# Second stage of a conditional MLP taken row by row, with one product of 512 and one of 256 columns per unit and two sums per tile

## Chip, core and metric

The kernel runs on one core of a Trainium2 chip. The metric is the device time of one execution in microseconds, median of the runs. Work is split over TensorE (PE, matrix products into PSUM), VectorE (DVE), ScalarE (ACT), GpSimd (POOL) and SyncE (SP, which issues nearly all DMAs).

## The reference, cut

32 rows of 256 tokens and 256 features; 1024 hidden features; 192 shared outputs and 64 outputs of one of 16 experts, chosen per row; all in fp32.

```python
h = jax.nn.gelu(jnp.einsum('bnd,hd->bnh', x, fc1_w) + fc1_b, approximate=False)
shared = jnp.einsum('bnh,sh->bns', h, fc2_w) + fc2_b
We = experts_w[indices]
be = experts_b[indices]
expert_x = jnp.einsum('bnh,bph->bnp', h, We) + be[:, None, :]
return x + jnp.concatenate([shared, expert_x], axis=-1)
```

## The kernel before

Every operand of a product is kept as a high part (rounded to TensorE's fp32r type) and a low part (what the rounding left). A product of two such operands is three products of TensorE: high x high, high x low, low x high.

**Blocks and stages.** A block is two rows: 512 tokens, four token tiles of 128. There are 16. The first stage (fc1, gelu) makes hidden features, transposed, in pairs of chunks (a chunk is 128 features, eight of them, four pairs, "quarters" below). Blocks 0 and 1 do it plainly, in `conv_chunk`: six products of 512 columns a chunk. Blocks 2 to 15 do it with seven groups of block products instead of eight (P1 to P7, `product`, six products of 256 columns each), in two rounds a block (`g` = 0 and 1, `t` counts them, 28 rounds). Between the groups ScalarE copies P1 and P5 out (`s1_copy`, `s5_copy`) and VectorE adds (`add_c11`, `add_v`, `add_c12`, `add_c22`); P4 is added last, so `product4(t - 1)` stands in the next round and waits for `add_c22`. ScalarE's gelus (`upper_pair`, `lower_pair`) leave two pairs a round in `gelu`; `pair_high` rounds them into `ht`, and POOL's `pair_lo` makes the low parts (in block 1 VectorE does it, `plain_low(4)` to `plain_low(7)`).

**The second stage** (`fc2_units(n, r, first, count)`, r a quarter) is cut into units: one token tile and one chunk, three products of 256 columns, weights from `w2t`. A quarter has eight units, two chunks by four tiles. Its sums stand in `acc_ps`, two banks, one for each row of the block. In `w2t` the columns of expert 0 stand left of the shared ones and those of expert 1 right, so each row reads 256 neighbouring columns. The units of block n - 1 fill the gaps of block n's rounds, two or three between each two groups. After the fourth quarter `drain` adds the sums to `resid`, which holds x plus the biases (`residual`, POOL). The sums of a row have one bank, drained while TensorE is at the other row.

**What sets the order.** All of it is written out by hand, one program per engine, with semaphores. The expert weights of a block are turned in VectorE (`experts_square`) into PSUM bank pair `tr_ps`, rounded by ScalarE (`experts_high`), and their low part made by VectorE (`experts_low`), in halves of four chunks for both rows at once. x of a later block goes the same way (`x_square`, `b_copy`, `x_high`, `x_low`, `x_sums_first`, `x_sums_last`, POOL's `x_sums_lo`). At the start POOL also forms four sums of first-stage weights (`weight_sum`), which VectorE turns (`s_square`), ScalarE rounds (`s_high`) and VectorE completes (`s_low`). SP's queue has, in this order, x of block 0, weights, experts 0, x of block 1 in pieces, expert biases 0, x of block 2, experts 1, and later the shared bias.

## Time and profile before

| | us |
|---|---|
| median of 3 runs (lowest to highest) | 363.62 (363.24 to 364.08) |
| the profiled execution | 363.34 |
| its span, first to last instruction | 361.5 |
| PE busy | 356.4 |
| ACT, DVE, POOL busy | 243.6, 224.0, 222.2 |

A product's busy time in the trace reaches into the next product's (a 256-column product is shown with 0.28 us while the products start 0.12 us apart), so distances from start to start are read, not durations. The granted clock of TensorE is 0.998 of full speed over the span. One execution's start times are in the rows further down, counted from the span's start.

### The profile page before, as it was taken

The numbers are of one execution on the slowest core, as the hardware profiler recorded it, in microseconds if no ns is written. First come the engines' busy times: TensorE is split into PE (matmuls) and PEld (weight loads), VectorE is DVE, ScalarE is ACT, GpSimd is POOL, SyncE is SP. The second block draws the span as 40 slices with busy tenths as digits, with TensorE's granted clock in tenths as the row PEclk, the third lists the DMA queues.
The fourth block names the chain that finished last, engine by engine and source line by source line (L and its number), as shares of the span: only waits on it lengthen the run. The fifth ranks groups of instructions, "written<-read, shape, count | busy, mean of one in ns | idle before, by whom it ended". The sixth has DMA issues, their size and how long they took to land.

```text
span 361.5 us, 7842 instructions
## 1 busy us (share of the span) xinstructions
PE 356.4 (99%) x2863; PEld 350.3 (97%) x2863; DVE 224.0 (62%) x367; ACT 243.6 (67%) x410; POOL 222.2 (61%) x100
## 2 busy tenths in 40 slices
PE   8999999999999999999999999999999999999996
PEld 6898999999999999999999999999999999999996
DVE  1797993937758285683937658395673938653241
ACT  3794865757849576694857759576794857757560
POOL 0079824676655677565676655677565577655381
PEclk9999999999999999999999999999999999999999
DMA  8869856361703426044261603526052321403011
GB/s 202 183 160 117 156 143 150 126 160 45 175 22 116 127 69 173 31 124 89 82 160 52 168 25 109 132 82 162 29 140 74 94 91 58 126 18 100 2 58 58
DMA packets 70447, 37.86 MB, mean 105 GB/s; under 512 B 43530, under 2 KB 70410, under 8 KB 70410
## 3 DMA queue, kind: packets, MB, share of 16 engines
q1 hardware_dynamic: 69792, 36.85, 40.8%
q10 hardware_dynamic: 618, 0.53, 0.6%
q8 instruction: 22, 0.36, 0.4%
q14 instruction: 15, 0.12, 0.1%
HBM read 28.97 MB, written 8.39 MB: 103 GB/s over the span
## 4 chain that ended last, share of the span: by engine, by line
PE 95%; issue 2%; POOL 1%; ACT 1%; DVE 0%; POOLq 0%
PE fc_ps L985 37%; PE acc_ps L1017 16%; PE acc_ps L1021 16%; PE acc_ps L1019 16%; PE fc_ps L961 6%; PE fc_ps L930 1%; POOL ht L353 1%; PE tr_ps L924 1%; PE fc_ps L968 1%; ACT ht L510 0%; ACT gelu L536 0%; DVE work L794 0%; DVE resid L819 0%; ACT w1t L430 0%; PE acc_ps L924 0%
## 5 line engine op out<-in xcount | busy, mean ns | idle before, releaser
L353 POOL TENSOR_TENSOR ht<-gelu,ht 128x1024 fp32r<-128x1024 f32 x60 | 144.5, 2408 | 121.3 <-ACT ht L510 121.3
L985 PE MATMUL fc_ps<-xt,w1t 128*128 128x256 f32 x1176 | 173.2, 283 | 0.0
L985 PEld LDWEIGHTS fc_ps<-xt,w1t 128*128 128x128 f32 x1176 | 155.3, 192 | 0.1
L1017 PE MATMUL acc_ps<-w2t,ht 128*128 128x256 f32 x512 | 144.9, 283 | 0.2 <-POOL ht L353 0.2
L1019 PE MATMUL acc_ps<-w2t,ht 128*128 128x256 f32 x512 | 144.9, 283 | 0.0
L1021 PE MATMUL acc_ps<-w2t,ht 128*128 128x256 f32 x512 | 144.9, 283 | 0.0
L1017 PEld LDWEIGHTS acc_ps<-w2t,ht 128*128 128x128 f32 x512 | 98.3, 192 | 0.6 <-POOL ht L353 0.3
L1019 PEld LDWEIGHTS acc_ps<-w2t,ht 128*128 128x128 f32 x512 | 98.3, 192 | 0.3
L1021 PEld LDWEIGHTS acc_ps<-w2t,ht 128*128 128x128 f32 x512 | 98.3, 192 | 0.0
L510 ACT ACTIVATE ht<-gelu 128x1024 fp32r<-128x1024 f32 x64 | 68.0, 1062 | 3.3
L496 ACT ACTIVATE work<-fc_ps 128x512 f32<-128x512 f32 x28 | 16.8, 600 | 57.4 <-PE fc_ps L985 57.4
L778 DVE TENSOR_TENSOR work<-fc_ps,work 128x512 f32<-128x512 f32 x28 | 19.4, 691 | 54.6 <-PE fc_ps L985 45.8
L346 POOL TENSOR_TENSOR resid<-resid,bias 128x1024 f32<-128x1024 f32 x16 | 38.9, 2432 | 1.5 <-DMA resid<-in_x 0.8
L787 DVE TENSOR_TENSOR work<-fc_ps,work 128x512 f32<-128x512 f32 x28 | 19.2, 687 | 32.0 <-PE fc_ps L985 32.0
L361 POOL TENSOR_TENSOR xt<-work,xt 128x1024 fp32r<-128x1024 f32 x14 | 33.6, 2402 | 7.7 <-ACT xt L500 7.7
L450 ACT ACTIVATE w2t<-tr_ps 128x512 fp32r<-128x512 f32 x32 | 18.8, 590 | 29.0 <-PE acc_ps L1021 29.0
L536 ACT ACTIVATE gelu<-work,b 128x512 f32<-128x512 f32 x56 | 37.1, 712 | 0.7 <-DVE work L794 0.7
L794 DVE TENSOR_TENSOR work<-fc_ps,work 128x512 f32<-128x512 f32 x28 | 19.3, 691 | 12.8 <-PE fc_ps L985 11.2
L548 ACT ACTIVATE gelu<-work,b 128x256 f32<-128x256 f32 x56 | 25.2, 501 | 0.0
L709 DVE TENSOR_TENSOR w2t<-tr_ps,w2t 128x512 fp32r<-128x512 f32 x32 | 22.0, 690 | 4.7 <-ACT w2t L450 3.2
L802 DVE TENSOR_TENSOR work<-fc_ps,work 128x512 f32<-128x512 f32 x28 | 19.1, 683 | 7.2 <-PE fc_ps L985 7.2
L553 ACT ACTIVATE gelu<-fc_ps,b 128x256 f32<-128x256 f32 x56 | 23.3, 469 | 0.0
(57 smaller groups left out, 279.5 us busy)
## 6 DMA issues: line engine op xcount, KB each, us to landing
pieces<-in_L_cond_experts_w SPq DMA_DIRECT2D x128, 64.0 KB, 2.0
out<-resid SPq DMA_DIRECT2D x32, 256.0 KB, 3.0
...
```

Of the source, the lines that this page charges most:

```text
L346: nc.gpsimd.tensor_tensor(rows, rows, bias[:, par, :, :].unsqueeze(2).to_broadcast([P, R, T, OUT]), ALU.add).then_inc(resid_ready, 1)
L353: nc.gpsimd.tensor_tensor(ht[:, slot, LO, :, :].rearrange("p k t -> p (k t)"), gelu[:, q % GELUS, :, :].rearrange("p k t -> p (k t)"), ht[ ...
L361: nc.gpsimd.tensor_tensor(xt[:, n % 2, X_T1:X_T4 + 1, LO, :], t_sum, xt[:, n % 2, X_T1:X_T4 + 1, HI, :].bitcast(FP32), ALU.subtract).then_ ...
L510: nc.scalar.activation(ht[:, q % PAIRS, HI, :, :].rearrange("p k t -> p (k t)"), gelu[:, q % GELUS, :, :].rearrange("p k t -> p (k t)"), A ...
L536: nc.scalar.activation(gelu[:, q % GELUS, j, :], upper[:, j, :], ACT.Gelu, bias=b1[:, k:k + 1]).then_inc(up_gelu, 1)
L548: nc.scalar.activation(gelu[:, q % GELUS, j, SEQ:2 * SEQ], c22[:, j, :], ACT.Gelu, bias=b1[:, k:k + 1]).then_inc(c22_gelu, 1)
L553: nc.scalar.activation(gelu[:, q % GELUS, j, 0:SEQ], fc1_ps[:, BANK_A[t % 2], j * SEQ:(j + 1) * SEQ], ACT.Gelu, bias=b1[:, k:k + 1]).then_ ...
L709: nc.vector.tensor_tensor(expert_columns(LO, ks), tr_ps[:, half, :].rearrange("p (k b c) -> p b k c", k=HALF, b=R), expert_columns(HI, ks) ...
L985: last = nc.tensor.matmul(fc1_ps[:, dst, j * SEQ:(j + 1) * SEQ], w1t[:, w, wv, ms], xt[:, n % 2, o, xv, :], start=(fresh and j == 0 and at ...
L1017: nc.tensor.matmul(dst, h_hi_t, w_hi, start=(r == 0 and u % (2 * T) == 0), stop=True, skip_group_check=True)
L1019: nc.tensor.matmul(dst, h_hi_t, w_lo, start=False, stop=True, skip_group_check=True)
L1021: last = nc.tensor.matmul(dst, h_lo_t, w_hi, start=False, stop=True, skip_group_check=True)
```

## The change

**Second stage by rows.** `fc2(i, first, count)` replaces `fc2_units`; i counts quarters of a row, eight a block: four of row 0, then four of row 1. A quarter has four units, two chunks by two tiles. A unit is two products: the high part of h against high and low weights side by side (512 columns, from two runs of 256 in `w2t`), and the low part of h against the high weights (256 columns) into the second half. So a tile has a bank of its own with two sums of 256, and `drain` adds both, one tile at a time, 8 adds for row 0 and 4 for row 1, where 2 and 1 stood. Both rows use the same two banks: the first units of a row wait, tile by tile, until the row ahead is drained.

**Storage.** `ht` has six pairs instead of four, since row 1 reads a pair later; `w1_piece` moves into `work`; the shared bias is kept once (`bias`), the expert biases apart (`e_bias`), and a residual is four instructions for a block, two for each row.

**Order.** In a round `product4(t - 1)` and both quarters i and i + 1 (i = 6 + 4 t) stand ahead of P1; then P1, P2, P5, P6 follow without units between; then three units, P3, two, P7, three. At the start six quarters of block 0 stand among the plain chunks (one chunk at the end without), the last two lead the first round; behind the last P4 stand ten quarters, forty units (thirty before). VectorE's and ScalarE's queues move the expert weights to halves by row; `drain(0, 0)` stands ahead of `plain_low(4)`; `x_square` or `experts_square` stands between `add_c12` and `add_c22`; `x_square` of block 3 stands ahead of `plain_low(7)`; ScalarE does `b_copy` and `x_high` ahead of `upper_pair` and `s1_copy`. POOL does `residual(0, 0)` ahead of all low parts, and SP loads the biases of block 0 ahead of the x pieces of block 1.

```diff
-        ht = sbuf("ht", [P, PAIRS, 2, 2, TOK], FP32R)
+        ht = sbuf("ht", [P, SLOTS, 2, 2, TOK], FP32R)
...
-        bias = sbuf("bias", [P, 2, R, OUT])
+        bias = sbuf("bias", [P, SHARED])
+        e_bias = sbuf("e_bias", [P, 2, R, PART])
...
+        w1_piece = work[:, 0:2048].rearrange("p (q k j) -> p q k j", q=Q, k=K)
...
-        def drained_at(n, b):
-
-            return 3 * n + 2 + b
+        def additions(b):
+
+            return 2 - b
+
+        def drained_at(n, b, t):
+
+            return 12 * n + 8 * b + 2 * additions(b) * (t + 1)
+
+        def fc2_end(n, b, r):
+
+            return R * PAIRS * n + PAIRS * b + r + 1
...
             numbers = load_experts(0)
+            load_expert_bias(0, numbers)
+            sp.dma_start(bias[:, :], fc2_b.rearrange("(o n) -> o n", o=1).to_broadcast([P, SHARED]))\
+                .then_inc(b2_loaded, 16)
             load_x_pieces(1)
...
+                    rows[:, :, 0:SHARED], rows[:, :, 0:SHARED],
+                    bias[:, :].unsqueeze(1).to_broadcast([P, T, SHARED]),
                     ALU.add).then_inc(resid_ready, 1)
+                nc.gpsimd.tensor_tensor(
+                    rows[:, :, SHARED:OUT], rows[:, :, SHARED:OUT],
+                    e_bias[:, par, b, :].unsqueeze(1).to_broadcast([P, T, PART]),
+                    ALU.add).then_inc(resid_ready, 1)
...
+            residual(0, 0)
             for r in range(PAIRS):
...
-            residual(0)
-            residual(1)
+            residual(0, 1)
+            for b in range(R):
+                residual(1, b)
...
             def drain(n, b):
-                if b == 0:
-                    dve.wait_ge(acc_filled, n + 1)
-                else:
-                    dve.wait_ge(fc2_pair, PAIRS * (n + 1))
-                dve.wait_ge(resid_ready, n + 1)
-                dst = resid[:, n % 2, b * T:(b + 1) * T, :]
-                src = acc_ps[:, b, :].rearrange("p (t o) -> p t o", t=T)
-                if b == 0:
-                    nc.vector.tensor_tensor(dst[:, :, 0:SHARED], src[:, :, PART:OUT],
-                                            dst[:, :, 0:SHARED], ALU.add).then_inc(drained, 1)
-                    nc.vector.tensor_tensor(dst[:, :, SHARED:OUT], src[:, :, 0:PART],
-                                            dst[:, :, SHARED:OUT], ALU.add).then_inc(drained, 1)
-                else:
-                    nc.vector.tensor_tensor(dst, src, dst, ALU.add).then_inc(drained, 1)
+
+                dve.wait_ge(resid_ready, 4 * n + 2 * b + 2)
+                for t in range(T):
+                    if t == 0:
+                        dve.wait_ge(tile_filled, R * n + b + 1)
+                    else:
+                        dve.wait_ge(fc2_done, fc2_end(n, b, PAIRS - 1))
+                    dst = resid[:, n % 2, b * T + t, :]
+                    for v in (HI, LO):
+                        src = acc_ps[:, t, v * OUT:(v + 1) * OUT]
+                        if v == LO:
+                            dve.wait_ge(drained, drained_at(n, b, t) - additions(b))
+                        if b == 0:
+                            nc.vector.tensor_tensor(dst[:, 0:SHARED], src[:, PART:OUT],
+                                                    dst[:, 0:SHARED], ALU.add)\
+                                .then_inc(drained, 1)
+                            nc.vector.tensor_tensor(dst[:, SHARED:OUT], src[:, 0:PART],
+                                                    dst[:, SHARED:OUT], ALU.add)\
+                                .then_inc(drained, 1)
+                        else:
+                            nc.vector.tensor_tensor(dst, src, dst, ALU.add).then_inc(drained, 1)
...
             experts_square(1, 0)
+            drain(0, 0)
             plain_low(4)
...
-            def fc2_units(n, r, first, count):
-
+            def fc2(i, first, count):
+
+                n, b, r = i // (R * PAIRS), i // PAIRS % R, i % PAIRS
                 q = PAIRS * n + r
                 for u in range(first, first + count):
-                    t, j = u // 2, u % 2
-                    b = t // T
+                    j, t = u // T, u % T
                     k = chunk_of(q, j)
                     if u == 0:
                         wait_h_lo(pe, q)
-                        if r % 2 == 0:
-                            pe.wait_ge(e_lo, 2 * n + r // 2 + 1)
-                        if q == 0:
+                        if r == 0:
+                            pe.wait_ge(e_lo, R * n + b + 1)
+                        if i == 0:
                             pe.wait_ge(w2_lo, 4)
-                    if r == 0 and n >= 1 and u in (0, T * 2):
-                        pe.wait_ge(drained, drained_at(n - 1, b))
-                    dst = acc_ps[:, b, (t % T) * OUT:(t % T + 1) * OUT]
-                    ts = slice(t * P, (t + 1) * P)
-                    h_hi_t = ht[:, q % PAIRS, HI, j, ts]
-                    h_lo_t = ht[:, q % PAIRS, LO, j, ts]
-                    w_hi = w2t[:, HI, k, fc2_columns(b)]
-                    w_lo = w2t[:, LO, k, fc2_columns(b)]
-                    nc.tensor.matmul(dst, h_hi_t, w_hi, start=(r == 0 and u % (2 * T) == 0),
-                                     stop=True, skip_group_check=True)
-                    nc.tensor.matmul(dst, h_hi_t, w_lo, start=False, stop=True,
-                                     skip_group_check=True)
-                    last = nc.tensor.matmul(dst, h_lo_t, w_hi, start=False, stop=True,
-                                            skip_group_check=True)
-                    if u == 7:
-                        last.then_inc(fc2_pair, 1)
-                    elif r == PAIRS - 1 and u == 3:
-                        last.then_inc(acc_filled, 1)
+                    if r == 0 and j == 0 and i > 0:
+
+                        pe.wait_ge(drained, drained_at(n - (1 - b), 1 - b, t))
+                    ts = slice((b * T + t) * P, (b * T + t + 1) * P)
+                    nc.tensor.matmul(acc_ps[:, t, :].rearrange("p (v o) -> p v o", v=2),
+                                     ht[:, q % SLOTS, HI, j, ts], w2t[:, :, k, fc2_columns(b)],
+                                     start=(k == 0), stop=True, skip_group_check=True)
+                    last = nc.tensor.matmul(acc_ps[:, t, OUT:2 * OUT],
+                                            ht[:, q % SLOTS, LO, j, ts],
+                                            w2t[:, HI, k, fc2_columns(b)],
+                                            start=False, stop=True, skip_group_check=True)
+                    if u == 3:
+                        last.then_inc(fc2_done, 1)
+                    elif r == PAIRS - 1 and u == 2:
+                        last.then_inc(tile_filled, 1)
...
-            fc2_units(0, 0, 0, 8)
+            fc2(0, 0, 4)
+            fc2(1, 0, 4)
             pe.wait_ge(x1_lo, D)
             conv_chunk(K)
-            for at in range(6):
-                fc2_units(0, 1 + at // 2, at % 2 * 4, 4)
-                conv_chunk(K + 1 + at)
+            conv_chunk(K + 1)
+            for at in range(4):
+                fc2(2 + at, 0, 4)
+                conv_chunk(K + 2 + at)
+            conv_chunk(2 * K - 2)
             conv_chunk(2 * K - 1)
 
             for n in range(PLAIN, BLOCKS):
                 for g in range(GROUPS):
                     t = group(n, g)
                     a = BANK_A[t % 2]
...
+                    i = 6 + 4 * t
+
+                    if t > 0:
+                        product4(t - 1)
+                    fc2(i, 0, 4)
+                    fc2(i + 1, 0, 4)
...
+            for i in range(6 + 4 * (LAST_T + 1), R * PAIRS * BLOCKS):
+                fc2(i, 0, 4)
```

TensorE, the head of the first round (t = 0), before; `fc_ps<-xt,w1t` are the groups P1, then P2, `acc_ps<-w2t,ht` the products of units:

```order
L985 MATMUL fc_ps<-xt,w1t 128x256 [waits conv_gelu]
L985 MATMUL fc_ps<-xt,w1t 128x256 x5
L1017 MATMUL acc_ps<-w2t,ht 128x256 [waits e_lo,plain_lo]
L1019 MATMUL acc_ps<-w2t,ht 128x256
L1021 MATMUL acc_ps<-w2t,ht 128x256
...
L985 MATMUL fc_ps<-xt,w1t 128x256 [waits c22_added]
L985 MATMUL fc_ps<-xt,w1t 128x256 x5
```

and now, from the last unit ahead of P1 to the first unit behind P6:

```order
L1043 MATMUL acc_ps<-w2t,ht 128x512
L1046 MATMUL acc_ps<-w2t,ht 128x256
L1015 MATMUL fc_ps<-xt,w1t 128x256 [waits conv_gelu,xb_lo]
L1015 MATMUL fc_ps<-xt,w1t 128x256 x5
L1015 MATMUL fc_ps<-xt,w1t 128x256 [waits conv_gelu]
L1015 MATMUL fc_ps<-xt,w1t 128x256 x5
L1015 MATMUL fc_ps<-xt,w1t 128x256 [waits s_lo,xt_lo]
L1015 MATMUL fc_ps<-xt,w1t 128x256 x5
L1015 MATMUL fc_ps<-xt,w1t 128x256 [waits s_lo,s1_copied]
L1015 MATMUL fc_ps<-xt,w1t 128x256 x5
L1043 MATMUL acc_ps<-w2t,ht 128x512 [waits drained,e_lo,plain_lo]
L1046 MATMUL acc_ps<-w2t,ht 128x256
```

The units between the groups are gone; the first units behind P6 wait (`drained`) for the tiles of the row ahead.

VectorE, behind the transposes of block 1's experts in the start (`L701`), before; `ht<-gelu,ht` is `plain_low`, `tr_ps<-w_in` is `s_square`, `w2t<-tr_ps,w2t` is `experts_low`:

```order
L701 STREAM_TRANSPOSE tr_ps<-pieces 128x4x4x32 [waits e_loaded1,t_added,xb_lo]
L729 TENSOR_TENSOR ht<-gelu,ht 128x1024 [waits h_hi]
L665 STREAM_TRANSPOSE tr_ps<-w_in 128x512 [waits s_added]
L709 TENSOR_TENSOR w2t<-tr_ps,w2t 128x2x4x64 [waits e_hi]
L671 TENSOR_TENSOR w1t<-tr_ps,w1t 128x512 [waits s_hi]
```

and now:

```order
L719 STREAM_TRANSPOSE tr_ps<-pieces 128x2x8x32 [waits e_loaded1,t_added,xb_lo]
L835 TENSOR_TENSOR resid<-acc_ps,resid 128x192 [waits tile_filled,resid_ready]
L838 TENSOR_TENSOR resid<-acc_ps,resid 128x64
L835 TENSOR_TENSOR resid<-acc_ps,resid 128x192 [waits drained]
L838 TENSOR_TENSOR resid<-acc_ps,resid 128x64
L835 TENSOR_TENSOR resid<-acc_ps,resid 128x192 [waits fc2_done]
...
L745 TENSOR_TENSOR ht<-gelu,ht 128x1024 [waits h_hi]
L683 STREAM_TRANSPOSE tr_ps<-w_in 128x512 [waits s_added]
L726 TENSOR_TENSOR w2t<-tr_ps,w2t 128x8x64 [waits e_hi]
L689 TENSOR_TENSOR w1t<-tr_ps,w1t 128x512 [waits s_hi]
```

Eight adds of the first drain, which wait for the fourth quarter of row 0 (`tile_filled`, `fc2_done`), have come ahead of all of this.

POOL, the head of its queue, before (`pair_lo`, `x_sums_lo`):

```order
L379 AFFINE_SELECT ident<-ident 128x128
L353 TENSOR_TENSOR ht<-gelu,ht 128x1024 [waits h_hi] x4
L361 TENSOR_TENSOR xt<-work,xt 128x4x256 [waits xt_hi]
```

and now:

```order
L394 AFFINE_SELECT ident<-ident 128x128
L356 TENSOR_TENSOR resid<-resid,bias 128x2x192 [waits b2_loaded,be_loaded0,x0_tr,x0_loaded0]
L360 TENSOR_TENSOR resid<-resid,e_bias 128x2x64
L368 TENSOR_TENSOR ht<-gelu,ht 128x1024 [waits h_hi] x4
L376 TENSOR_TENSOR xt<-work,xt 128x4x256 [waits xt_hi]
```

The residual of row 0, with its wait for both biases, stands ahead of the four low parts.

## Rows read from the trace of the kernel before

**Rows 1.** Page of the profile: busy time of each engine; the chain that ended last.

```profile
PE 356.4 (99%) x2863; PEld 350.3 (97%) x2863; DVE 224.0 (62%) x367; ACT 243.6 (67%) x410; POOL 222.2 (61%) x100
...
PE 95%; issue 2%; POOL 1%; ACT 1%; DVE 0%; POOLq 0%
```

**Rows 2.** Timeline, 149.8 to 151 us: start, us, engine, line, operation, out<-in.

```profile
149.89 0.28 PE L1017 MATMUL acc_ps<-w2t,ht 128*128 128x256 f32 x1
...
150.25 0.28 PE L1017 MATMUL acc_ps<-w2t,ht 128*128 128x256 f32 x1
...
150.42 0.53 DVE L814 TENSOR_TENSOR resid<-acc_ps,resid 128x384 f32<-128x384 f32 x1
...
150.88 0.27 DVE L816 TENSOR_TENSOR resid<-acc_ps,resid 128x128 f32<-128x128 f32 x1
```

**Rows 3.** TensorE by stretch, line 961 alone: us, PE busy (count), weight loads, clock, DMA, GB/s.

```profile
11.40:21.04 9.64, 9.64 (x42) 7.78 (x42) 1.00 0.78 171
23.92:25.30 1.38, 1.38 (x6) 0.94 (x6) 1.00 0.47 118
```

**Rows 4.** Timeline: the one wait of TensorE after 21 us.

```profile
343.15 2.41 POOL L353 TENSOR_TENSOR ht<-gelu,ht 128x1024 fp32r<-128x1024 f32 x1 [5.63 <-ACT ht L510]
...
345.67 0.19 PEld L1017 LDWEIGHTS acc_ps<-w2t,ht 128*128 128x128 f32 x1 [0.34 <-POOL ht L353]
...
345.89 0.28 PE L1019 MATMUL acc_ps<-w2t,ht 128*128 128x256 f32 x1
```

**Rows 5.** VectorE's groups by form: busy us, mean ns of one | idle before.

```profile
L720 DVE STREAM_TRANSPOSE tr_ps<-pieces 128x512 f32<-128x512 f32 x30 | 19.7, 700 | 0.1
...
L709 DVE TENSOR_TENSOR w2t<-tr_ps,w2t 128x512 fp32r<-128x512 f32 x32 | 22.0, 690 | 4.7 <-ACT w2t L450 3.2
...
L724 DVE TENSOR_TENSOR work<-tr_ps,work 128x256 f32<-128x256 f32 x28 | 11.7, 418 | 0.5
...
L819 DVE TENSOR_TENSOR resid<-acc_ps,resid 128x512 f32<-128x512 f32 x16 | 10.9, 680 | 0.7 <-PE acc_ps L1021 0.7
...
L729 DVE TENSOR_TENSOR ht<-gelu,ht 128x1024 fp32r<-128x1024 f32 x4 | 6.6, 1658 | 1.6 <-ACT ht L510 1.4
...
L816 DVE TENSOR_TENSOR resid<-acc_ps,resid 128x128 f32<-128x128 f32 x16 | 4.4, 274 | 0.0
```

**Rows 6.** Timeline: a seventh product of a round and the add behind it.

```profile
159.97 0.88 PE L985 MATMUL fc_ps<-xt,w1t 128*128 128x256 f32 x6
...
160.89 0.69 DVE L802 TENSOR_TENSOR work<-fc_ps,work 128x512 f32<-128x512 f32 x1 [0.51 <-PE fc_ps L985]
```

**Rows 7.** Timeline: a weight load that waited for VectorE.

```profile
8.84 1.29 DVE L659 TENSOR_TENSOR w1t<-acc_ps,w1t 128x512 fp32r<-128x512 f32 x2 [0.45 <-ACT w1t L430]
...
10.18 0.19 PEld L968 LDWEIGHTS fc_ps<-xt,w1t 128*128 128x128 f32 x1 [0.30 <-DVE w1t L659]
```

**Rows 8.** Timeline: ScalarE's copy of P5, and the low part that follows in POOL.

```profile
156.21 0.60 ACT L496 ACTIVATE work<-fc_ps 128x512 f32<-128x512 f32 x1 [0.33 <-PE fc_ps L985]
...
159.55 2.41 POOL L353 TENSOR_TENSOR ht<-gelu,ht 128x1024 fp32r<-128x1024 f32 x1 [2.93 <-ACT ht L510]
```

**Rows 9.** Timeline of the start, SP and POOL.

```profile
12.95 2.02 SPq L269 DMA_DIRECT2D pieces<-in_x  x4
...
18.16 2.41 POOL L353 TENSOR_TENSOR ht<-gelu,ht 128x1024 fp32r<-128x1024 f32 x1 [16.68 <-ACT ht L510]
...
21.23 2.41 POOL L353 TENSOR_TENSOR ht<-gelu,ht 128x1024 fp32r<-128x1024 f32 x1 [0.66 <-ACT ht L510]
...
27.30 2.65 POOL L353 TENSOR_TENSOR ht<-gelu,ht 128x1024 fp32r<-128x1024 f32 x1 [0.58 <-ACT ht L510]
```

**Rows 10.** DMA view, 26 to 42 us: issues, KB each, median us to landing.

```profile
bias<-in_L_cond_fc_b SPq DMA_DIRECT2D x1, 384.0 KB, 12.0
```

**Rows 11.** Timeline: a VectorE instruction with two operands in SBUF beside one of POOL.

```profile
29.90 2.40 POOL L361 TENSOR_TENSOR xt<-work,xt 128x1024 fp32r<-128x1024 f32 x1
...
31.26 2.13 DVE L729 TENSOR_TENSOR ht<-gelu,ht 128x1024 fp32r<-128x1024 f32 x1 [1.44 <-ACT ht L510]
```

More of the change, by code:

```diff
@@ L272, in store @@
             def store(n, b):
[L273 removed]
+                sp.wait_ge(drained, drained_at(n, b, T - 1))
                 ts = slice(b * T, (b + 1) * T)
@@ L306, in _ @@
             load_x_pieces(3)
-            sp.wait_ge(e_sq, 2)
+            sp.wait_ge(e_sq, R)
             numbers = load_experts(2)
-            sp.wait_ge(resid_ready, 1)
+            sp.wait_ge(x_sq, 2 * D)
+            load_x_pieces(4)
+            sp.wait_ge(resid_ready, 4)
             load_expert_bias(2, numbers)
-            for n in range(1, BLOCKS):
-                if n >= 2:
-                    store(n - 2, 1)
+            store(0, 0)
+            for n in range(PLAIN, BLOCKS):
                 if n + 3 <= LAST:
@@ L408, in _ @@
                     if g == 1:
-                        residual(n)
+                        for b in range(R):
+                            residual(n, b)
             pair_lo(pair_at(LAST_T, 0))
@@ L587, in _ @@
             conv_chunk(4)
-            for half in range(2):
-                experts_high(0, half)
+            for b in range(R):
+                experts_high(0, b)
             conv_chunk(5)
@@ L837, in _ @@
             dve.wait_ge(w1_lo, 2 * D)
-            for half in range(2):
-                experts_square(0, half)
-            for half in range(2):
-                experts_low(0, half)
+            for b in range(R):
+                experts_square(0, b)
+            for b in range(R):
+                experts_low(0, b)
             dve.wait_ge(e_lo, 2)
@@ L870, in _ @@
             s_square(2)
-            experts_square(1, 1)
             s_low(2)
-            drain(0, 0)
-            drain(0, 1)
             plain_low(6)
+            dve.wait_ge(s_lo, 4)
+            for d in range(D):
+                x_square(PLAIN + 1, d)
             plain_low(7)
```

203 lines of the change are left out of this document (98 added, 105 removed).

## The prediction

> **What bounds the kernel now.** I read the page's shares first: TensorE is busy 356.4 us of a span of 361.5, and the chain that ended last is 95% TensorE [rows 1]. A busy TensorE can still be slowed by its products' own gaps, so next comes the pitch, from start to start. Three products of the second stage start 0.12 us apart, so one unit (one token tile, one hidden chunk, three products of 256 columns) takes 150.25 - 149.89 = 0.36 us [rows 2]. The 512-column products of the start take 9.64 / 42 = 0.2295 us each, six of them 1.38 us [rows 3]. Twice 256 columns cost 0.240 us and once 512 cost 0.2295: a product has a fixed part of some 0.010 us. From 21.04 us, the end of the first of those stretches, TensorE has one hole, 0.34 us at 345.67 [rows 4]. So nothing but TensorE sets the time, every product saved counts in full, and every new hole counts in full too.
>
> **What the change does, part by part.** The sum is made against the profiled execution, 363.34 us (span 361.5, 1.84 around it); the median of the runs is 363.62.
>
> *Products.* A unit becomes one product of 512 and one of 256: 0.2295 + 0.120 = 0.3495 us instead of 0.360. There are 512 units (the 512 of L1017): 512 x 0.0105 = **-5.4**. The trace holds no product whose moving columns lie in two runs; by the nearest rows a unit lies between 0.360 (two runs cost what two products cost) and 3 x (0.2295 - 0.120) = 0.3285 (no fixed part left), a saving of 0 to 16.1. I take 0.3495 because L961 streams the same 512 columns in the same type.
> The Trainium skill ("TensorE: Matmul & The Clock Gate", Back-to-back issue gap) gives N / 2.4 plus about 2.5 ns. By it a unit saves one fixed part of 2.5 ns, as an estimate 1.3 us in all, and the sum below would be 4.1 us higher. The rows differ: 256 columns take 13 ns, not 2.5, over their 107.
>
> *The rounds of the loop.* A round has seven groups of six products (0.72 each) and 16 units: 5.04 + 5.76 = 10.80 before, 5.04 + 5.59 = 10.63 now. The new order is safe where it leaves more than a microsecond: the sums of a row are drained under P1, P2, P5, P6 (2.88 us); eight adds for row 0 take 4 x 0.34 + 4 x 0.21 = 2.2 us, four for row 1 take 4 x 0.42 = 1.7 (widths between and beside [rows 5]). One place is tight. Only three units now stand between P7 and P4, where three units, P1 and two more stood. P7 started at 159.97 and VectorE's add began at 160.89, ended at 161.58, 1.61 after P7's start [rows 6]. VectorE to weight load takes 10.18 - 10.13 = 0.05 [rows 7], so P4's load can start at 1.66; TensorE gets there at 0.72 + 3 x 0.3495 - 0.12 = 1.65. The transposes placed between the two adds fit: third add 0.69 and 0.70 of transpose end 0.1 before P7 has. I take 0.02 a round, 28 rounds: **+0.6**, between 0 and 0.1 a round.
> Costed at nothing: the second quarter of a round now leads, so its low part is wanted earlier. ScalarE's copy of P5 started at 156.21 and that low part ended at 161.96, 5.75 later [rows 8]; the copy now comes 5.9 into a round (P4, eight units, P1, P2, P5, 0.2 of ends), so the part is ready 1.0 into the next one, and wanted at 0.72 + 1.40 - 0.21 = 1.9. That 0.9 is its cover. The doubled adds and the split residuals fill idle time of VectorE (62% busy) and POOL (61%) [rows 1]; the row-wise expert weights keep their size.
>
> *The start.* Here cover is lost. Before, quarter 1's low part (POOL, 21.23 to 23.64) had until 25.30, since eight units and a chunk stood ahead of it [rows 9]. Now four units do: TensorE arrives at 21.04 + 1.40 = 22.44. And POOL first does `residual(0, 0)`, which waits for both biases. SP issues them from 12.95 on, some 1 us for the expert rows; the shared bias took 12.0 us to land at 384 KB [rows 10], a quarter of it is left, so 3.0 by proportion: it lands near 17.3. Half a residual in two instructions is about 1.4 us (an estimate from 2.40 for 1024 columns). POOL is free at 18.7 to 18.9 instead of 18.16, quarter 1's low part ends at 23.8, and POOL to product takes 345.77 - 345.56 = 0.21 [rows 4] (345.77 is 0.12 ahead of the second product's start). So quarter 1 starts at 24.0, 1.5 late; if the bias lands 2.5 later, 4.0 late. (The x pieces of block 1, put back by the biases by some 1.5 us in SP's queue, are wanted for chunk 8, which is 1.5 later itself.) Chunk 8 ends at 26.8; the low part of quarter 3 started 2.0 after chunk 8's end (27.30 against 25.30), now 28.8, ends 31.2; quarter 3 runs 31.4 to 32.8. Without waits its end is 21.04 + 16 x 0.3495 + 3 x 1.38 = 30.8.
> Behind it hangs VectorE. `drain(0, 0)` stands ahead of `plain_low(4)` in its queue, so four low parts of block 1, eight transposes and low parts of the weight sums, the expert low part, two transposes and five small sums of block 3 all wait for quarter 3; and quarter 8 waits for `drain(0, 1)` behind them all. From the first add: 2.2 for the first drain, 4 x 1.66, 6 x 0.70, 5 x 0.69, 5 x 0.42, then 1.7 for the second drain: 20.3 us [rows 5]. An instruction that waits for nothing starts 0.07 before the one ahead has ended (150.42 + 0.53 against 150.88 [rows 2]); 28 such steps take off 2.0, waits on ScalarE, above all for the fourth weight sum, add 0.7: 19.0. The first tile's sums are full 0.18 before quarter 3 ends, 32.65, so the second drain ends at 51.65 and TensorE sees it at 51.8. TensorE alone would be there at 21.04 + 32 x 0.3495 + 8 x 1.38 + 2.88 + 0.35 = 46.5. **+5.3**. A low part of two operands in SBUF took 2.13 when POOL was at work and ended 1.09 after POOL's instruction did (31.26 + 2.13 against 29.90 + 2.40 [rows 11]); with POOL out of the way it is 1.1, so the term lies between 3.1 (four at 1.1) and 7.8 (bias 2.5 late).
> The Trainium skill ("SBUF — State Buffer", Who interferes with whom) says that a VectorE instruction with two SBUF inputs and a GpSimd instruction that reads SBUF exclude each other for a whole instruction; the row agrees. By it the new adds, with one operand in PSUM, are not slowed.
>
> *The end.* Ten quarters stand behind the last P4, with no group of products between a row's last quarter and the next row's first. Both tiles must be drained there. Row 1 of block 14: the tile is full 0.18 before the quarter ends, two dependent adds 0.87, hops of 0.04 (160.85 to 160.89 [rows 6]) and 0.17 (0.05 to the load, 0.12 to its product): 0.9 of waiting, then 0.4 more for tile 1 (its adds take 0.83 more, TensorE does one unit of 0.35): **+1.3**. Row 0 of block 15 has four adds a tile, 1.05 and 0.9: **+1.6**. The last drain is four adds, 1.63 from 0.14 before the last slot ends; one of 0.68 stood there (L819), starting 0.19 after it: **+0.6**. The hole at 345.67 goes: **-0.3**.
>
> Sum: -5.4 + 0.6 + 5.3 + 1.3 + 1.6 + 0.6 - 0.3 = +3.7, so 363.34 + 3.7 = **367.0 us**.
>
> **Rivals.**
> *The gaps vanish (faster).* While 512 columns stream, the next weights load in full; if the fixed part is what a load costs that doesn't fit under its stream, a unit takes 0.3285 and 10.7 more are saved: 356.3. It beats the kernel before from 0.341 a unit down. For it: no row shows long and short products in turn. Against it: the 42 long products in a row had the same room for their loads and took 0.2295, not 0.219. Chance 0.12.
> *VectorE's queue doesn't decide the start (no difference).* If the second drain is there when quarter 8 is, only the 2.0 us up to quarter 3 remain, 3.3 less: 363.7. It needs a chain of 15.7 instead of 19.0 us. Chance 0.10.
> *The biases land late.* +2.5: 369.5. For it: the 12.0 us of the same transfer. Against it: it is now a quarter as long and issued behind a queue that was nearly empty. Chance 0.09.
> *P4 waits in every round.* If the transpose ahead of the add comes late, by a quarter of a microsecond, 28 x 0.23 more: 373.4. Against it: 0.1 us of room by the rows. Chance 0.09.
> *Only a small fixed part is saved*, 2.5 ns a unit instead of 10.5: 371.1. Chance 0.03, since the 512-column rows speak against it. The Trainium skill's gap, cited above, is that case.
>
> **How the numbers follow.** My sum, 367.0, has 0.57. With the second and third rival that is 0.76, and the lower half of the fourth's prices belongs to it too, some 0.80; the range that they span is 363.6 to 370.4, which takes in the bounds of the start (3.1 to 7.8) as well. Below 0.2% (0.7 us), which is about what a measurement of this kernel can tell from no change: faster 0.14 (the first rival and a little of my own case), same 0.10 (the second), slower 0.76.
>
> **What the profile after would show.** Units 0.35 apart (right) or 0.33 or 0.36 (wrong). A round of 10.63 to 10.65 and no wait for the fourth add. Holes of TensorE at 21 to 24 us released by POOL's low part, at some 31 us, at 48 to 52 us released by VectorE's adds or its ScalarE successors, 5 us in all; VectorE without idle time from 33 to 51 us. Two holes after the last P4, 1.3 and 1.6. If there are no holes at 48 to 52 us, the chain of VectorE was wrong; if the rounds differ from 10.6, the pitch or the tight place was.

## The result, and the profile after

The changed kernel takes 370.15 us (369.82 to 371.26, median of 4 runs) against 363.82 for the kernel before in the same session: a ratio of 1.0182, 95% interval 1.0156 to 1.0208. It is slower, as forecast, but by 6.3 us instead of 3.4. The profiled execution took 370.4 us, its span is 368.4.

The page of the kernel after, shares and TensorE's clock (the answer to [rows 1]; the last line is the clock in 40 slices of 9.2 us):

```profile
PE 357.8 (97%) x2351; PEld 324.8 (88%) x2351; DVE 254.0 (69%) x511; ACT 246.9 (67%) x410; POOL 235.0 (64%) x148
...
PEclk9999989999999999999999999999999999999999
```

TensorE is the bound still, with 512 products fewer and a busy time that is 1.4 us longer. The sixth slice of the clock was a 9 before. TensorE's timeline, after (start, time, line, [idle before, releaser]): the first and the last row are P1, P2, P5 and P6 of the second and of the last round; the two at 82.55 and 93.24 are one round apart, with units between (where [rows 2] had three products 0.12 apart).

```profile
61.16 3.04 PE L1015 MATMUL fc_ps<-xt,w1t 128*128 128x256 f32 x24
...
82.55 3.04 PE L1015 MATMUL fc_ps<-xt,w1t 128*128 128x256 f32 x24
85.42 0.40 PE L1043 MATMUL acc_ps<-w2t,ht 128*128 128x512 f32 x1
85.65 0.28 PE L1046 MATMUL acc_ps<-w2t,ht 128*128 128x256 f32 x1
85.77 0.40 PE L1043 MATMUL acc_ps<-w2t,ht 128*128 128x512 f32 x1
...
93.24 3.04 PE L1015 MATMUL fc_ps<-xt,w1t 128*128 128x256 f32 x24
...
339.19 3.04 PE L1015 MATMUL fc_ps<-xt,w1t 128*128 128x256 f32 x24
```

One unit shows 0.35, but the round tells it closer: from 61.16 to 339.19 there are 26 rounds, 10.693 us each, and (10.693 - 7 x 0.72) / 16 = 0.3533. No wait stands in these 26 rounds.

The same view at the start (first the long stretch of the plain chunks) and behind the last P4:

```profile
12.47 9.81 PE L991 MATMUL fc_ps<-xt,w1t 128*128 128x512 f32 x42
...
24.76 0.50 PE L1043 MATMUL acc_ps<-w2t,ht 128*128 128x512 f32 x1 [0.73 <-POOL ht L368]
...
49.05 0.97 PE L1015 MATMUL fc_ps<-xt,w1t 128*128 128x256 f32 x6 [0.42 <-ACT work L507]
51.53 0.47 PE L1043 MATMUL acc_ps<-w2t,ht 128*128 128x512 f32 x1 [1.51 <-DVE resid L842]
...
52.23 0.80 PE L1043 MATMUL acc_ps<-w2t,ht 128*128 128x512 f32 x1
...
350.82 0.47 PE L1043 MATMUL acc_ps<-w2t,ht 128*128 128x512 f32 x1 [0.78 <-DVE resid L842]
357.91 0.47 PE L1043 MATMUL acc_ps<-w2t,ht 128*128 128x512 f32 x1 [0.92 <-DVE resid L838]
358.74 0.50 PE L1043 MATMUL acc_ps<-w2t,ht 128*128 128x512 f32 x1 [0.24 <-DVE resid L838]
...
364.03 0.28 PE L1046 MATMUL acc_ps<-w2t,ht 128*128 128x256 f32 x1
```

Quarter 8 starts at 51.53, released by the second drain. POOL's first residual and VectorE's chain from the first add of the first drain to the second drain:

```profile
18.49 1.02 POOL L356 TENSOR_TENSOR resid<-resid,bias 128x384 f32<-128x384 f32 x1 [17.01 <-DMA bias<-in_L_cond_fc_b]
...
33.46 0.36 DVE L835 TENSOR_TENSOR resid<-acc_ps,resid 128x192 f32<-128x192 f32 x1 [2.57 <-PE acc_ps L1046]
...
44.35 0.69 DVE L689 TENSOR_TENSOR w1t<-tr_ps,w1t 128x512 fp32r<-128x512 f32 x1 [0.67 <-ACT w1t L449]
...
50.51 1.67 DVE L842 TENSOR_TENSOR resid<-acc_ps,resid 128x256 f32<-128x256 f32 x4
```

Behind the start of quarter 8 products are slow: 0.80 instead of 0.40 for 512 columns. The windows of that stretch say why (columns: time, busy time and count of PE, PEld, DVE, ACT, POOL, then the granted clock, DMA share, GB/s):

```profile
51.00:52.00 1.00, 0.47 (x2) 0.30 (x2) 0.97 (x3) 0.69 (x1) 0.23 (x1) 0.97 0.29 56
52.00:53.00 1.00, 0.93 (x4) 0.67 (x3) 1.00 (x3) 0.00 (x0) 1.00 (x1) 0.50 0.00 0
53.00:54.00 1.00, 1.00 (x6) 0.90 (x5) 0.97 (x2) 0.00 (x0) 1.00 (x1) 0.50 0.78 262
54.00:55.00 1.00, 1.00 (x7) 1.00 (x7) 0.00 (x0) 0.00 (x0) 0.15 (x1) 0.50 0.00 0
55.00:56.00 1.00, 1.00 (x7) 0.87 (x7) 0.80 (x2) 0.00 (x0) 0.00 (x0) 0.83 0.31 48
```

For some 3 us TensorE was granted half its clock, 1.2 of 2.4 GHz. That was in no term of the forecast.

Forecast and measurement by marks of TensorE (the forecast's later marks are carried on with its own units and rounds):

| mark | forecast | after | miss, from the mark before |
|---|---|---|---|
| quarter 0 starts | 21.04 | 22.35 | |
| quarter 1 starts | 24.0 | 24.76 | |
| quarter 8 starts | 51.8 | 51.53 | -0.3 |
| P1 of the second round (16 units, 3 groups later) | 59.55 | 61.16 | +1.9 |
| P1 of the last round (26 rounds later) | 59.55 + 26 x 10.65 = 336.45 | 339.19 | +1.1 |
| end of the span | 361.5 + 3.7 = 365.2 | 368.4 | +0.5 |

The sum is 3.2; 0.2 more lies around the span.

### The profile page after: what moved, and what is told of

Read it like the earlier page. It is cut to its first block, busy times and chain, and to the rows that moved or that the text cites. A ratio compares the mean times of both kernels' runs of the same rounds, so it can differ in the third digit from the quotient of the medians.

```text
span 368.4 us, 7042 instructions
## 1 busy us (share of the span) xinstructions
PE 357.8 (97%) x2351; PEld 324.8 (88%) x2351; DVE 254.0 (69%) x511; ACT 246.9 (67%) x410; POOL 235.0 (64%) x148
## 4 chain that ended last, share of the span: by engine, by line
PE 85%; DVE 5%; POOL 2%; SPq 2%; DMA 2%; issue 2%; ACT 1%; DVEq 0%; POOLq 0%
PE fc_ps L1015 38%; PE acc_ps L1043 31%; PE acc_ps L1046 16%; POOL ht L368 2%; DVE resid L842 1%; DMA bias<-in_L_cond_fc_b 1%; DVE ht L745 1%; DMA resid<-in_x 1%; SPq L261 1%; DVE resid L835 1%; ACT ht L528 1%; ACT gelu L540 1%; SPq L300 0%; SPq L245 0%; PE fc_ps L991 0%
## 5 line engine op out<-in xcount | busy, mean ns | idle before, releaser
L1043 PE MATMUL acc_ps<-w2t,ht 128*128 128x512 f32 x512 | 188.4, 402 | 4.5 <-DVE resid L842 2.3
L1015 PE MATMUL fc_ps<-xt,w1t 128*128 128x256 f32 x1176 | 159.9, 283 | 0.4 <-ACT work L507 0.4
L1046 PE MATMUL acc_ps<-w2t,ht 128*128 128x256 f32 x512 | 144.2, 282 | 0.0
L1043 PEld LDWEIGHTS acc_ps<-w2t,ht 128*128 128x128 f32 x512 | 97.0, 190 | 25.7 <-issue 4.0
L1046 PEld LDWEIGHTS acc_ps<-w2t,ht 128*128 128x128 f32 x512 | 97.5, 191 | 0.2
L835 DVE TENSOR_TENSOR resid<-acc_ps,resid 128x192 f32<-128x192 f32 x64 | 22.8, 356 | 39.4 <-PE acc_ps L1046 38.3
L356 POOL TENSOR_TENSOR resid<-resid,bias 128x384 f32<-128x384 f32 x32 | 38.1, 1190 | 17.0 <-DMA bias<-in_L_cond_fc_b 17.0
L507 ACT ACTIVATE work<-fc_ps 128x512 f32<-128x512 f32 x28 | 16.8, 599 | 39.9 <-PE fc_ps L1015 39.9
L842 DVE TENSOR_TENSOR resid<-acc_ps,resid 128x256 f32<-128x256 f32 x64 | 25.6, 420 | 13.1 <-PE acc_ps L1046 12.0
L803 DVE TENSOR_TENSOR work<-fc_ps,work 128x512 f32<-128x512 f32 x28 | 19.4, 691 | 17.9 <-PE fc_ps L1015 17.9
L810 DVE TENSOR_TENSOR work<-fc_ps,work 128x512 f32<-128x512 f32 x28 | 19.4, 692 | 15.1 <-PE fc_ps L1015 15.1
L513 ACT ACTIVATE work<-fc_ps 128x512 f32<-128x512 f32 x28 | 16.8, 599 | 15.9 <-PE fc_ps L1015 15.9
L465 ACT ACTIVATE w2t<-tr_ps 128x512 fp32r<-128x512 f32 x32 | 18.7, 588 | 7.2 <-DVE tr_ps L719 5.5
L719 DVE STREAM_TRANSPOSE tr_ps<-pieces 128x512 f32<-128x512 f32 x32 | 22.8, 717 | 0.1
```

Of the source, the lines that this page charges most:

```text
L356: nc.gpsimd.tensor_tensor(rows[:, :, 0:SHARED], rows[:, :, 0:SHARED], bias[:, :].unsqueeze(1).to_broadcast([P, T, SHARED]), ALU.add).then_ ...
L835: nc.vector.tensor_tensor(dst[:, 0:SHARED], src[:, PART:OUT], dst[:, 0:SHARED], ALU.add)\
L842: nc.vector.tensor_tensor(dst, src, dst, ALU.add).then_inc(drained, 1)
L1015: last = nc.tensor.matmul(fc1_ps[:, dst, j * SEQ:(j + 1) * SEQ], w1t[:, w, wv, ms], xt[:, n % 2, o, xv, :], start=(fresh and j == 0 and at ...
L1043: nc.tensor.matmul(acc_ps[:, t, :].rearrange("p (v o) -> p v o", v=2), ht[:, q % SLOTS, HI, j, ts], w2t[:, :, k, fc2_columns(b)], start=(k ...
L1046: last = nc.tensor.matmul(acc_ps[:, t, OUT:2 * OUT], ht[:, q % SLOTS, LO, j, ts], w2t[:, HI, k, fc2_columns(b)], start=False, stop=True, s ...
```

## Experiments

**Is the fused product worth 5.4 us?** *e1_split* undoes it alone and keeps the order:

```diff
-nc.tensor.matmul(acc_ps[:, t, :] ..., ht HI, w2t[:, :, k, ...])          # 512 columns
+for v in (HI, LO):
+    nc.tensor.matmul(acc_ps[:, t, v * OUT:(v + 1) * OUT], ht HI, w2t[:, v, k, ...])
```

> Only the 512-column product is undone: it is issued as two of 256 columns into the two sums; the row-wise order, the waits and the drains stay. My account of the trace after: a unit took 0.3536 us there, not 0.3495, so the fusion saved 512 x 0.0064 = 3.3 us; undone, the time is 370.2 + 3.3 - 0.2 (32 units less of waiting ahead of the second drain) = 373.3 us (373.0 to 373.8), units 0.360 apart. If the forecast's 0.0105 a unit was right after all and the rounds lose time elsewhere: 375.4. If a moving operand in two runs costs as much as two products: 370.2.

373.37 us (372.41 to 374.52), and a round of 10.80 exactly:

```profile
61.07 3.04 PE L1015 MATMUL fc_ps<-xt,w1t 128*128 128x256 f32 x24
...
71.87 3.04 PE L1015 MATMUL fc_ps<-xt,w1t 128*128 128x256 f32 x24
```

So the fusion gives 373.37 - 370.15 = 3.2 us, and everything else in the change costs 373.37 - 363.84 = 9.5. Four kernels look for the reason why a unit is not 0.3495; all but e6_pairs have one execution each.

*e5_plain_columns* streams 512 columns in one run: `w2t[:, :, k, ...]` becomes `w1t[:, W_A11, HI, :]`.

> Only what the 512-column product streams is changed: 512 columns that lie in one run (a slice of the first stage's weights) instead of two runs of 256 from the second stage's; so the second stage's sums leave out its own weights there. If the two runs are what makes a unit 0.3536 us instead of 0.3495, units stand 0.3495 apart and the time is 370.2 - 2.1 = 368.1 us. If the change between long and short products is it, units stay at 0.3536 and the time at 370.2.

Measured 370.33, a round of 10.693 (26 of them): two runs are not the reason.

*e6_pairs* issues both tiles' 512 columns, then both tiles' 256.

> Only the order within a quarter is changed: for each chunk both tiles' products of 512 columns, then both of 256, instead of 512, 256, 512, 256. If a product costs more behind one of the other length, two units take 2 x 0.3495 = 0.699 us instead of 0.707: 370.2 - 2.1, and 0.23 more at each of the two last drains, since tile 0 ends 0.23 later: 368.5 us (368.2 to 368.8). If the lengths' order is nothing to it: 370.6.

372.25 us (370.70 to 372.84), a round of 10.70: half as many changes of length give nothing back, and waits grew (0.70 ahead of P6, 1.02 and 1.15 for the drains at the end).

*e13_long_alone* leaves out the 256-column product, *e14_short_twice* issues it twice.

> The 256-column product of each unit is left out (so the sums lack the low part of the hidden values), which leaves runs of 512-column products in the second stage. If its 512-column products cost 0.2295 us like the first stage's and only the change between lengths costs 0.004 a unit, they stand 0.2295 apart; if a 512-column product of the second stage costs 0.2333 by itself, 0.233. Its time is no measure (TensorE has 61 us less, and waits appear): some 310 to 325 us.

> The 256-column product of each unit is issued twice (so the low part is added twice). If 256 columns behind 256 cost 0.120 us as in the kernel before, a unit takes 0.3533 + 0.120 = 0.4733 us, a round 5.04 + 7.57 = 12.61, and the kernel 512 x 0.120 = 61.4 us more: 431.6. If the long product is slower wherever a short one precedes it, the pitch is the same 0.4733; if the short product behind a long one is the cheaper one, the second one costs more than 0.120: 0.475 and more.

TensorE's timeline of e13_long_alone has eight long products in a row between P4 and P1:

```profile
102.47 2.00 PE L1043 MATMUL acc_ps<-w2t,ht 128*128 128x512 f32 x8
104.31 3.06 PE L1015 MATMUL fc_ps<-xt,w1t 128*128 128x256 f32 x24
```

1.84 / 8 = 0.230: among its own kind the long product costs in the second stage what it costs in the first. e14_short_twice has 22 rounds between these two rows:

```profile
62.48 3.03 PE L1015 MATMUL fc_ps<-xt,w1t 128*128 128x256 f32 x24
...
339.10 3.03 PE L1015 MATMUL fc_ps<-xt,w1t 128*128 128x256 f32 x24
```

Its round is 12.574, so the extra short product costs (12.574 - 10.693) / 16 = 0.1175. The time, 425.5, was not the 431.6 expected, for three reasons: each added product is cheaper than 0.120 (1.3 us in all), the clock stayed at 1.00, and waits are shorter (0.46 ahead of quarter 8 instead of 1.51); that these three make up the whole 6.1 is not shown. So a unit that has both lengths costs 0.0033 us more than 0.230 + 0.120, the prices of each length among its own kind. Since e6 did not get any of it back, what makes it stays open; no run varies the weight loads.

**Does the half clock follow from the hole ahead of quarter 8?** *e2_fill* puts 15 unused bf16 products there (`if t == 0: fill(15)` ahead of `fc2(i + 2, 0, 3)`).

> Fifteen products of 256 bf16 columns (on the identity, result unused, some 1.6 us) fill TensorE's hole between P6 of the first round and quarter 8 (49.77 to 51.53 us). If the fall of the granted clock to 0.50 from 52 to 55 us follows from that hole, the clock stays at 1.00, quarter 8 to the end of P3 takes 1.78 us instead of 3.43, and the time is 370.2 - 1.8 = 368.4 us (368.1 to 368.8). If the clock falls for another reason (the work of other engines, the moment in the program): 370.2 and the same 0.50 in these rows. If the added products hold quarter 8 back: 370.5 to 371.5.

369.07 us (368.31 to 369.50). Windows of e2_fill, same columns, and then TensorE's start of quarter 0, of quarter 8 and of the second round:

```profile
50.00:51.00 1.00, 1.00 (x11) 0.86 (x11) 0.96 (x3) 0.19 (x1) 0.00 (x0) 1.00 1.05 237
51.00:52.00 1.00, 1.00 (x9) 0.83 (x8) 0.93 (x4) 0.87 (x1) 0.05 (x1) 1.00 0.40 84
52.00:53.00 1.00, 0.89 (x5) 0.55 (x4) 1.00 (x3) 0.00 (x0) 1.00 (x1) 1.00 0.00 0
53.00:54.00 1.00, 1.00 (x10) 0.95 (x9) 1.00 (x2) 0.00 (x0) 1.00 (x1) 1.00 0.68 232
```

```profile
22.67 0.50 PE L1049 MATMUL acc_ps<-w2t,ht 128*128 128x512 f32 x1 [1.61 <-POOL ht L368]
...
51.71 0.47 PE L1049 MATMUL acc_ps<-w2t,ht 128*128 128x512 f32 x1
...
59.98 3.04 PE L1021 MATMUL fc_ps<-xt,w1t 128*128 128x256 f32 x24
```

VectorE and POOL do the same there as before, quarter 8 starts 0.18 later (51.71), and the clock stays at 1.00 (over the span 0.998 to 1.000 in all four executions, where the kernel after had 0.993 to 0.995 in all four). So without this hole the clock does not fall here. From quarter 8 to the next round's P1 it takes 59.98 - 51.71 = 8.27 instead of 61.16 - 51.53 = 9.63: the half clock cost 1.36. I had expected 1.8, having counted the second tile's wait for its drain (0.35) as clock.

**The two holes at the end.** *e4_end* sums row 0 of the last block in banks 0 and 2 of `fc1_ps`:

```diff
+def tile_sum(n, b, t):
+    if (n, b) == (LAST, 0):
+        return fc1_ps[:, (BANK_A[(LAST_T + 1) % 2], BANK_B)[t], :]
+    return acc_ps[:, t, :]
```

> The last block's row 0 is summed in two banks of the first stage that are free by then, so that TensorE waits for no drain behind the last P4. The holes there were 2.96 us together (0.9 to 1.6 each row): 370.2 - 2.9 = 367.3 us (367.0 to 367.6). If an engine behind them (ScalarE's GELU or POOL's low part of the last quarters) ends later than the drains did, part of it comes back: 368 to 369.5.

368.07 us (367.52 to 369.54), 2.1 less. All drain waits are gone; one new wait stands there, for POOL, which had the last residuals ahead of the last low parts (e8_both turns them round, and the wait is gone):

```profile
354.72 0.50 PE L1054 MATMUL fc_ps<-w2t,ht 128*128 128x512 f32 x1 [0.58 <-POOL ht L373]
```

**The start, three repairs.** *e3_start*: on VectorE `plain_low(4)` ahead of `drain(0, 0)`, and the second drain and the first adds ahead of block 3's transposes and sums; POOL's first residual later.

> Order of the start alone: POOL's first residual goes behind its second low part; on VectorE the low part of quarter 4 goes ahead of the first drain, and the second drain and the first round's adds go ahead of the transposes and sums of block 3 (ScalarE's copies of block 3 behind its two copies of the first round). My account: the start's waits (about 4.2 us after 22 us, of them 1.8 ahead of quarter 8 and 0.6 ahead of P6) fall to 1 or less and the half clock (1.8) goes with them: 370.2 - 3.2 - 1.8 = 365.2 us (364.6 to 366.2). If VectorE's total work and not its order sets the start, P3, P7 or P4 of the first round wait instead: 367.5 to 369. If the forecast's 5.3 us for the start were the size: 363.2.

371.24 us (370.58 to 371.94). My account of what to move was wrong. VectorE and TensorE of e3_start:

```profile
32.92 2.43 DVE L749 TENSOR_TENSOR ht<-gelu,ht 128x1024 fp32r<-128x1024 f32 x1 [1.44 <-ACT ht L529]
...
36.42 0.47 PE L1053 MATMUL acc_ps<-w2t,ht 128*128 128x512 f32 x1 [1.40 <-DVE resid L842]
...
59.04 0.98 PE L1025 MATMUL fc_ps<-xt,w1t 128*128 128x256 f32 x6 [2.09 <-DVE work L822]
```

VectorE's idle time ahead of the first drain could not be filled: ScalarE finished that quarter's high part only at 32.9, and the low part then took 2.43 beside POOL instead of 1.27. So the first drain was late, quarter 4 waited, and the clock fell to 0.50 between 38 and 42 us. The second drain was indeed in time; but block 3's sums now stood ahead of `add_c22`, and P4 waited 2.09.

*e7_start2*: chunk 8 between quarters 0 and 1, POOL's residual behind its fourth low part, `plain_low(6)` and `(7)` on POOL; *e8_both* adds the end, with POOL's last low parts ahead of the last residuals.

> Another repair of the start alone. TensorE: chunk 8 goes between quarters 0 and 1. POOL: the first residual goes behind its fourth low part, and POOL takes the low parts of the last two plain quarters from VectorE. VectorE's order stays as in the changed kernel. My account: quarter 0's 0.24, quarter 1's 0.9, the wait ahead of quarter 8 and its second tile (1.8 + 0.35) and the half clock (1.4) go, the 0.4 to 0.6 ahead of P6 stays: 370.2 - 4.4 = 365.8 us (365.2 to 366.8). VectorE has 2.4 us less ahead of the first round's adds, which is what it was late by; if its chain is longer than I read it, P3 waits and 367 to 368.5 result. If TensorE loses its clock in another hole: 1.4 more.

> The start as in e7_start2, the last block's row 0 in two free banks as in e4_end, and POOL's last two low parts ahead of the last residuals (they held the last row but one back by 0.6 us in e4_end). 365.8 - 2.9 = 362.9 us (362.2 to 363.9), which would be 0.9 below the kernel before. If the start's repair fails: 365 to 366.

371.29 (370.88 to 372.73) and 369.34 (367.58 to 370.21). TensorE got to the first round 1.7 us earlier in e7 (P1 at 44.62 against 46.30). But 1.5 of that is not the edit's: in this execution the long first stretch of products started at 10.99 instead of 12.47, with nothing changed ahead of it. Quarter 8 started at 51.95 all the same. POOL, VectorE and TensorE of e7_start2:

```profile
46.44 2.36 POOL L377 TENSOR_TENSOR ht<-gelu,ht 128x1024 fp32r<-128x1024 f32 x1 [0.93 <-ACT ht L539]
...
46.88 2.20 DVE L751 TENSOR_TENSOR work<-b_rows 128x256 f32<-128x256 f32 x1 [0.76 <-ACT b_rows L509]
...
51.95 0.61 PE L1052 MATMUL acc_ps<-w2t,ht 128*128 128x512 f32 x1 [2.89 <-DVE resid L853]
```

The low part that POOL took over held VectorE: a sum that takes 0.40 took 2.20 and ended 0.28 behind POOL's instruction. (The Trainium skill, "SBUF — State Buffer", Who interferes with whom, has this exclusion; the row agrees.) VectorE had two low parts less (2.7 us in the kernel after), but from its first add (31.80) to the end of the second drain (52.60) it took 20.8 us instead of 18.7: besides these 1.8, it waited 0.93 for a weight sum of POOL and 0.66 and 0.76 for ScalarE. Work moved to POOL came back as waiting, and TensorE's holes grew to 1.14 ahead of P6 and 2.89 ahead of quarter 8. It was the forecast's own step, VectorE's queue, that I had lost sight of.

*e9_start3* moves what stands ahead of the second drain in VectorE's queue and is not wanted yet (block 3's last low part and the transposes of block 1's second expert weights go behind `add_c22(0)` too):

```diff
-plain_low(6); x_square(3, 0); x_square(3, 1); plain_low(7)
-x_sums_first(3); x_low(3, 0); x_sums_last(3)
 drain(0, 1); add_c11(0)
+plain_low(6)
 add_v(0)
+x_square(3, 0); x_square(3, 1)
 add_c12(0); add_c22(0)
+plain_low(7); x_sums_first(3); x_low(3, 0); x_sums_last(3)
```

with ScalarE's `b_copy(3)`, `x_high(3)` behind `s5_copy(0)`, the x pieces of block 1 ahead of the biases, and chunk 8 and POOL's residual as in e7. *e10_both3* adds the end of e8.

> A third repair of the start, for what the first two showed: VectorE's queue, not TensorE's, sets when the second drain is done (quarter 8 starts at 51.4 to 52.6 us whatever TensorE's holes before it are). Now the second drain and the first round's four adds stand ahead of all transposes and sums of block 3 and of two low parts (each add put where TensorE wants it), ScalarE copies block 3 behind its copies of the first round, chunk 8 goes between quarters 0 and 1 with block 1's pieces of x issued ahead of the biases, and POOL's first residual goes behind its fourth low part. Terms: quarter 8 wants the drain at some 48 us and VectorE can end it at 46.5 to 47; left are 0.4 ahead of P6 and some 0.7 ahead of the second round's drain; the half clock (1.4) is not met. 370.2 - 4.6 = 365.6 us (364.9 to 366.8). If VectorE's work and not its order is the limit, a wait of 1.5 to 3 ahead of P3, P4 or quarter 12 stands there: 367.5 to 370.

> e9_start3 with the last block's row 0 in two free banks and POOL's last two low parts ahead of the last residuals, as in e8_both, where TensorE had no hole behind its last P4. 365.6 - 2.9 = 362.7 us (362.0 to 363.9), against 363.9 before. If the start fails as above: 364.7 to 367.

369.11 (369.00 to 369.23) and 365.94 (363.75 to 366.15). Quarter 8 starts without a wait in e9 (first row), and the second round's P1 5.1 us earlier than in the kernel after (second row):

```profile
48.27 0.40 PE L1073 MATMUL acc_ps<-w2t,ht 128*128 128x512 f32 x1
...
56.06 2.31 PE L1045 MATMUL fc_ps<-xt,w1t 128*128 128x256 f32 x18
```

So the order of VectorE's queue set the start of quarter 8 (e7 had the same edits to chunk 8 and to POOL's residual, and quarter 8 still waited), and the start is mended. Most of it was lost again in that second round, which took 14.55 us instead of 10.69. ScalarE, then TensorE, of e9_start3:

```profile
55.30 1.06 ACT L517 ACTIVATE xt<-work 128x1024 fp32r<-128x1024 f32 x1 [3.54 <-DVE work L745]
56.66 0.60 ACT L465 ACTIVATE w2t<-tr_ps 128x512 fp32r<-128x512 f32 x1 [0.30 <-DVE tr_ps L724]
57.16 1.33 ACT L554 ACTIVATE gelu<-work,b 128x512 f32<-128x512 f32 x2
...
59.48 0.58 ACT L507 ACTIVATE work<-fc_ps 128x512 f32<-128x512 f32 x1
...
60.11 0.98 PE L1045 MATMUL fc_ps<-xt,w1t 128*128 128x256 f32 x6 [1.74 <-ACT work L507]
```

ScalarE waited for VectorE's late sums with the ready gelus queued behind; so its copy of P1 was late, TensorE waited 1.74 ahead of P6, and the clock was 0.50 from 61 to 64 us. In e10_both3 the same hole stands ahead of P6, and the clock falls behind it in the profiled execution. Nine of e10's twelve executions have a granted clock of 0.992 to 0.995 over the span and take 365.82 to 366.15; three have 1.000 and take 363.75 to 363.97. So the fall does not come in every execution of the same kernel; whether the hole was the same in those three no profile shows. *e11_best* puts `upper_pair(0)` ahead of `x_sums_high(3)` and runs the last quarter tile by tile; *e12_early_x* moves block 1's x ahead of the second row's expert weights on VectorE and ScalarE.

> e10_both3 with two more edits. ScalarE's GELU of the first round's upper pair goes ahead of its copy of block 3's sums: in e10_both3 it stood behind that copy and behind an expert copy, both of which waited for VectorE until 55 and 57 us, so that the copy of P1's sum came late and TensorE waited 1.74 us ahead of P6 of the second round, and lost its clock there (2.5 us at 0.50, of which half is lost, and 0.24 ahead of the next P4). And the last quarter runs tile by tile, so that the last drain of tile 0 starts 0.35 earlier. If the account of the start is right: 365.9 - 1.7 - 1.3 - 0.2 - 0.35 = 362.3 us (361.8 to 363.2), 1.6 below the kernel before. If the half clock comes from something else than that hole: 363.6 to 364.

> e11_best, and on VectorE and ScalarE block 1's transposes, copies and low parts go ahead of the second row's expert weights, which are wanted only by quarter 4. TensorE waited 1.0 us for block 1's low part ahead of chunk 8 in e10_both3; ScalarE's copies of it move by 0.7, so this should save 0.6 to 0.8 if nothing behind them (the second drain) sets the start now: 361.6 us (361.1 to 362.6). If VectorE's queue up to the second drain is still what decides: as e11_best.

e11_best: 362.56 us (361.95 to 363.15), ratio to the kernel before 0.9962, interval 0.9948 to 0.9977: 0.4% below the kernel before, and so faster than both kernels. Its page has no 8 left in the clock's line (first), and on its timeline two waits of TensorE remain behind its first product (second):

```profile
PEclk9999999999999999999999999999999999999999
```

```profile
24.48 0.73 PE L1029 MATMUL fc_ps<-xt,w1t 128*128 128x512 f32 x2 [0.99 <-DVE xt L766]
64.17 0.98 PE L1053 MATMUL fc_ps<-xt,w1t 128*128 128x256 f32 x6 [0.23 <-DVE work L831]
```

e12_early_x: 363.76 us (362.83 to 364.28), ratio 0.9992 (0.9981 to 1.0004). The 0.99 is gone, but ScalarE's copy of the moved expert weights now waits for VectorE ahead of quarter 2's high part (first row), and TensorE for that quarter (second):

```profile
24.36 0.60 ACT L472 ACTIVATE w2t<-tr_ps 128x512 fp32r<-128x512 f32 x1 [0.94 <-DVE tr_ps L732]
...
29.00 0.50 PE L1089 MATMUL acc_ps<-w2t,ht 128*128 128x512 f32 x1 [0.95 <-POOL ht L373]
```

## Why the prediction was right in sign and wrong in size

Two steps failed: the price of a unit in the products' term, and the clock, which the sum left out at the start's holes. The measured 370.15 lies inside the stated 363.6 to 370.4, but near its upper end, which stood for late biases and for waits of P4; they are not what made up the miss.

- **Products, -5.4: the mis-sized term.** It measures 512 x 0.0067 = -3.4 from the rounds (10.800 to 10.693), 3.2 from e1. The step that failed is "I take 0.3495 because L961 streams the same 512 columns in the same type" [rows 3]: each length's price came from runs of its own kind, the unit has both. In its place e1 and the rounds show 0.3533 us a unit. (By the Trainium skill, "TensorE: Matmul & The Clock Gate", Back-to-back issue gap, an estimate of -1.3 stood beside it; the measurement lies between, 6.7 ns a unit where the Trainium skill gives 2.5. That section gives its formula for the isolated product, and says that in a stream of weight loads and products both set the spacing, which the prediction passed over.)
- **The rounds, +0.6: too much.** No P4 waits, rounds are all alike, so the tight place read from [rows 6] had room. Products and rounds together miss by 1.4.
- **The start, +5.3: right in mechanism, its mark in part by luck.** Quarter 8 was to start at 51.8 behind VectorE's queue and started at 51.53; from 33.46 to 52.18 VectorE had but one break above 0.2, the 0.67, and its chain took 18.7 us (19.0 forecast). e9 confirms that the queue's order decides. Marks ahead of it were read worse: the shared bias took 4.2 us to land instead of 3.0, so POOL's first low part started at 19.89, not 18.8, quarter 1 at 24.76, not 24.0, and the chain's first add at 33.46, not 32.65. So the second drain ended at 52.18, 0.5 later than forecast; the mark fits because quarter 8 does not wait for the whole drain, as the forecast had it, but for the first tile's half. Of quarter 0's 1.31 only 0.24 is a wait, which the sum left out. The other 1.07 is where the long first stretch started, 12.47 instead of 11.40, and that differs from execution to execution: in e2, with nothing changed ahead of it, it started at 11.25, and quarter 1, behind POOL, still at 25.02.
- **The step that is missing: the clock.** "5 us in all" of holes was written down without a word on what TensorE's clock does behind them. It cost 1.36 (e2). In its place the windows show 0.50 for some 3 us. The second tile's wait, 0.35, is priced at the end and has no term at quarter 8; there the mark, taken for the whole drain, makes up for 0.3 of it.
- **The end, +1.3 and +1.6: right.** From the end of the last P4 (347.05) 40 units alone would start their last product at 361.06; it started at 364.03, 2.97 later. e4 gets 2.1 of it back, and e11 shows no wait there. The last drain was +0.7 for +0.6.
- **The rivals.** "P4 waits in every round" and "the gaps vanish" did not happen. That VectorE's queue would not decide the start is refuted by the 1.51 ahead of quarter 8 and by e9. "The biases land late" came in part: about 1 us, of which 0.8 reached the chain's first add. "Only a small fixed part is saved" was too far the other way: 2.5 ns a unit, and 6.7 were measured.
